# Wide attention: merged block maxima in fp32, rounded by ScalarE and turned one unit later

## The reference, cut to what matters

```python
B, S, D_MODEL = (4, 1024, 128)
NUM_HEADS, HEAD_DIM = (16, 64)
q, k, v = split_heads(x @ w_q), split_heads(x @ w_k), split_heads(x @ w_v)
attn = jnp.einsum('bnqd,bnkd->bnqk', q, k) * HEAD_DIM ** (-0.5)
attn = jax.nn.softmax(attn, axis=-1)
o = jnp.einsum('bnqk,bnkd->bnqd', attn, v)
```

## Time and profile before

| | |
|---|---|
| median of 3 runs | 3791.35 us (3790.73 to 3795.37) |
| profiled execution | 3790.09 us, of which the span is 3788.5 us |
| busy in the span | TensorE 2937.9 us (78%), VectorE 2389.0 (63%), ScalarE 1842.5 (49%), POOL 1520.5 (40%) |
| wide attention's loop, 95 to 1330 us | TensorE 1202.13 us, POOL 1123.42, VectorE 807.68, ScalarE 659.68 |
| additions of POOL | 448, 2.35 us each |

### The profile page before, as it was taken

The page is one execution under the profiler, slowest core; times in us unless marked ns, Lnnn a source line. Parts: engine busy times, 40 slices in busy tenths (PEclk is TensorE's granted clock), DMA queues, the critical chain, the costliest instruction groups (busy, mean ns, idle before and its releaser), DMA issues. The chain is left out here.

```text
span 3788.5 us, 67132 instructions
## 1 busy us (share of the span) xinstructions
PE 2937.9 (78%) x21195; PEld 1318.0 (35%) x21196; DVE 2389.0 (63%) x3399; ACT 1842.5 (49%) x2929; POOL 1520.5 (40%) x1110
## 2 busy tenths in 40 slices
PE   3999999999999953899645999999579420839983
PEld 1333333333333353333321222222246320526661
DVE  5666666666666535888857898999433454334532
ACT  2555555555555500444633898898534430443331
POOL 0899898989989910100000000101046307520000
PEclk9999999999999976999856999999789755969955
DMA  2011111111111151100023222222111212130012
GB/s 79 29 44 51 44 51 44 50 39 44 51 44 51 37 177 56 48 1 0 2 81 95 47 56 55 48 56 53 50 50 45 63 59 93 50 94 14 8 41 64
DMA packets 269545, 195.38 MB, mean 52 GB/s; under 512 B 150485, under 2 KB 212942, under 8 KB 268488
## 3 DMA queue, kind: packets, MB, share of 16 engines
q1 hardware_dynamic: 260936, 178.09, 16.5%
q0 software_dynamic: 8512, 16.11, 1.3%
HBM read 105.02 MB, written 69.19 MB: 46 GB/s over the span
## 5 line engine op out<-in xcount | busy, mean ns | idle before, releaser
L329 POOL TENSOR_TENSOR attn_esum<-attn_esum,attn_prob 128x1024 f32<-128x1024 f32 x384 | 903.8, 2354 | 41.4 <-ACT attn_prob L480 17.9
L540 DVE TENSOR_REDUCE attn_half_max<-attn_peek 128x2 f32<-128x1024 f32 x512 | 627.5, 1226 | 398.0 <-PE attn_peek L380 394.3
L480 ACT ACTIVATE attn_prob<-attn_score 128x1024 f32<-128x1024 f32 x512 | 512.6, 1022 | 297.1 <-PE attn_score L363 297.1
L844 DVE TENSOR_REDUCE attn_half_max<-attn_peek 128x2 f32<-128x1024 f32 x512 | 588.1, 1218 | 51.2 <-PE attn_peek L763 51.2
L827 ACT ACTIVATE attn_prob<-attn_score 128x512 f32<-128x512 f32 x1024 | 556.0, 596 | 111.3 <-PE attn_score L777 98.6
L410 PE MATMUL attn_acc<-attn_prob,attn_v 128*64 128x512 f32 x2048 | 487.9, 597 | 0.1
L793 PE MATMUL attn_acc<-attn_prob,attn_v 128*32 128x256 f32 x4096 | 339.1, 404 | 8.9 <-ACT attn_out L819 7.4
L1685 POOL DMA_INDIRECT sorted_x<-attn_sent_rows,attn_send x64 | 62.7, 979 | 599.8 <-PE attn_score L777 564.5
L763 PE MATMUL attn_peek<-attn_ke,attn_qe 48*128 48x512 bf16 x1024 | 208.7, 404 | 44.2 <-DMA attn_ke<-k 32.0
L777 PE MATMUL attn_score<-attn_qe,attn_ke 49*128 49x512 bf16 x1024 | 206.7, 400 | 36.9 <-DMA attn_qe<-max 29.7
L380 PE MATMUL attn_peek<-attn_hi 64*128 64x512 f16 x1024 | 200.2, 388 | 44.2 <-DVE attn_half_max L540 44.2
(11 more groups left out here) (452 smaller groups left out, 4661.4 us busy)
## 6 DMA issues: line engine op xcount, KB each, us to landing
attn_xb<-attn_x_all SPq DMA_DIRECT2D x66, 256.0 KB, 2.5
attn_invB<-inv SPq DMA_DIRECT2D x64, 256.0 KB, 4.0
o<-attn_out SPq DMA_DIRECT2D x32, 512.0 KB, 2.7
out_o<-o SPq DMA_DIRECT2D x8, 2048.0 KB
mix_f<-picked SPq DMA_DIRECT2D x16, 512.0 KB, 7.2
experts_x<-sorted_x SPq DMA_DIRECT2D x112, 65.0 KB
attn_qe<-q SPq DMA_DIRECT2D x192, 32.0 KB
attn_ke<-k SPq DMA_DIRECT2D x192, 32.0 KB
```

The source lines that it names most:

```text
L329: nc.gpsimd.tensor_tensor(own, before, prob[:, u % NPROB, :, :], ALU.add).then_inc(added, 1)
L480: nc.scalar.activation(prob[:, u % NPROB, :, :], score[:, u % 2, :, :], ACT.Exp).then_inc(exped, 1)
L540: V.tensor_reduce(half_max[:, half, :, t], peek[:], AX.X, ALU.max, negate=True).then_inc(maxed, 1)
L844: V.tensor_reduce(half_max[:, half, PAIR * pair:PAIR * (pair + 1), t], peek[:, m % NPEEK, :, :], AX.X, ALU.max, negate=True).then_inc(maxe ...
```

## The change

`merge` writes its result as fp32 to a new buffer `both`. ScalarE copies it, rounded to bf16, into `nmax` (`round_maxima`). A new function `turn` holds the transpose; it waits for the copy, and `TURN_AT` puts it one unit behind the merge, behind the maximum of that unit. ScalarE's copy stands in front of the odd unit's exponential of the step that begins there. The merge now also waits for the copy of the item before. The stage's first merge and turn stand in the prologue, one maximum apart.

```diff
+    TURN_AT = {u + 1: c for u, c in MAX_AT.items()}
...
+        both = st.sb("both", [P, NC, heads, TPC])
...
+            def round_maxima(i, c):
+                act.wait_ge(merged, NC * i + c + 1)
+                nc.scalar.activation(nmax[:, c, 0:heads * TPC].rearrange("p (h t) -> p h t", h=heads), both[:, c, :, :], ACT.Copy
+                                     ).then_inc(rounded, 1)
...
+                    if TURN_AT.get(u) == 1:
+                        round_maxima(i, 1)
+                    elif TURN_AT.get(u) == 0 and not final:
+                        round_maxima(i + 1, 0)
                     exp(i, u + 1, first)
...
             def merge(i, c, any_before):
                 dve.wait_ge(maxed, U * i + (c + 1) * PER_HALF)
                 tiles = slice(c * TPC, (c + 1) * TPC)
-                V.tensor_tensor(nmax[:, c, 0:heads * TPC].rearrange("p (h t) -> p h t", h=heads), half_max[:, 0, :, tiles],
-                                half_max[:, 1, :, tiles], ALU.min).then_inc(merged, 1)
-                dve.wait_ge(merged, NC * i + c + 1)
+                if any_before:
+                    dve.wait_ge(rounded, NC * (i - 1) + c + 1)
+                V.tensor_tensor(both[:, c, :, :], half_max[:, 0, :, tiles], half_max[:, 1, :, tiles], ALU.min).then_inc(merged, 1)
+
+            def turn(i, c, any_before):
+                dve.wait_ge(rounded, NC * i + c + 1)
                 if any_before:
                     dve.wait_ge(shift_out, DMA * BLOCKS * (NC * (i - 1) + c + 1))
                 V.transpose(nmaxT[:, c, :], nmax[:, c, :]).then_inc(max_ready, 1)
...
+                    if TURN_AT.get(u) == 1:
+                        turn(i, 1, not first)
+                    elif TURN_AT.get(u) == 0 and not final:
+                        turn(i + 1, 0, True)
```

More of the change, by code:

```diff
@@ L203, in wide_attention_stage @@
         small = st.ps("small", [P, CH])
-        names = ("w_loaded", "w_stored", "all_hi", "all_lo", "consts", "made", "hi_ready", "lo_ready", "v_ready", "peeked", "maxed", "merged",
+        names = ("w_loaded", "w_stored", "all_hi", "all_lo", "consts", "made", "hi_ready", "lo_ready", "v_ready", "peeked", "maxed", "merged", "rounded",
                  "max_ready", "scored", "exped", "added", "weighed", "read_out", "summed", "sums_read", "inverted", "normed")
-        (w_loaded, w_stored, all_hi, all_lo, consts, made, hi_ready, lo_ready, v_ready, peeked, maxed, merged,
+        (w_loaded, w_stored, all_hi, all_lo, consts, made, hi_ready, lo_ready, v_ready, peeked, maxed, merged, rounded,
          max_ready, scored, exped, added, weighed, read_out, summed, sums_read, inverted, normed) = (st.sem(n) for n in names)
@@ L527, in _ @@
             act.wait_ge(all_lo, 3 + BATCH)
+            act.wait_ge(consts, 4)
+            round_maxima(0, 0)
             exp(0, 0, True)
@@ L569, in then @@
                 def then(u):
-                    c = MAX_AT.get(u)
-                    if c == 1:
+                    if MAX_AT.get(u) == 1:
                         merge(i, 1, not first)
-                    elif c == 0 and not final:
+                    elif MAX_AT.get(u) == 0 and not final:
                         merge(i + 1, 0, True)
+                    if TURN_AT.get(u) == 1:
+                        turn(i, 1, not first)
+                    elif TURN_AT.get(u) == 0 and not final:
+                        turn(i + 1, 0, True)
                 for s in range(STEPS):
@@ L599, in _ @@
                     merge(0, 0, False)
+                elif m == PER_HALF:
+                    turn(0, 0, False)
             iterations(dve, body)
```

## The result

The changed kernel takes 3780.24 us (median of 14 runs, 3771.61 to 3789.92) against 3791.07 us before (median of 14, 3788.29 to 3798.21): 10.8 us less. The ratio is 0.997, with a 95% interval of 0.9961 to 0.9978. Forecast were 3781.5 us and 9.8 us. The profiled execution took 3775.64 us, with a span of 3774.0. One of the 21 runs of the kernel before that stand beside four of the experiments took 7794.95 us, at a granted clock of 0.511 instead of 0.88, and the ratios leave it out.

The account below looks back on a forecast made before the run. TensorE was taken to wait about 1.0 us in almost every item for a maximum delayed behind VectorE's merge, which sits out POOL's addition. 10.1 us gained less 0.3 for late shifts gave 9.8 us: 3781.5 us, range 3777 to 3789.

Parts of the forecast that it names:

- The merge: VectorE's merge, with two SBUF inputs, still waits for POOL's running addition in fp32: 2.16 us again, gain 0.
- The size: At half 1, take_low and maximum 4 come 0.34 us earlier, so look 5 does too: 10.1 us over 30 waits.
- The late shift: Half 0's shift reaches its matmul 0.1 us late; 0.8 us of lateness are absorbed at look 5, so no cost.
- The one late shift of the beginning: In the prologue and first item the shift may be late with nothing absorbing it: 0 to 1.4 us once, 0.3 taken.
- Freed by fp32: Rival: fp32 output frees the merge to 0.17 us, look 5 no longer waits: 32 us gained, 3759.5 us; chance 0.10.
- The transpose waits for POOL: Rival: the moved transpose is held by POOL's addition, shift 1.0 us late at one half: 3 us gained, 3788.5; chance 0.06.
- Nothing gained: Rival: take_low starts no earlier, held by something the trace puts down to the transpose: 3791.35 us; chance 0.04.
- slower: Rival: second half's transpose held to 725.8 us, its shift matmul waits 2.3 us an item: 3850 us; chance 0.06 with lesser mishaps.

Follow-up runs that it names:

- the fp32 merge in its old place: Changed kernel with the transpose put back directly behind the merge, fp32 output and ScalarE's rounding kept: 3794.82 us against 3790.51 before, ratio 1.0007.
- one-input merge: Kernel before with the merge as a tensor_reduce over the two key halves, bf16 output, transpose in its old place: 3755.26 us against 3790.51, ratio 0.9908.
- the run with two units: Kernel before with half 1's transpose one unit later and half 0's two units later: 3802.24 us against 3787.85, ratio 1.0042.
- bf16 merge: Kernel before with the transpose alone moved one unit later, no ScalarE rounding: 3780.88 us against 3790.51, ratio 0.9974.
- three roundings: Changed kernel with two more ScalarE copies of the same columns in front of each rounding: 3780.01 us against 3790.94 before, ratio 0.9973.

## Why the prediction was right

**The merge.** Predicted: held as before, in fp32 as in bf16. It was, 1610 ns on average against 1664 and 0.03 us behind POOL's addition. Here the rule of the Trainium skill ("SBUF — State Buffer", "Who interferes with whom") was the one that counted, for the trace of before was silent on the fp32 form; the traces of the changed kernel and of the fp32 merge in its old place now agree with it. The one-input merge took 171 ns beside the same additions; the same section of the Trainium skill says that a VectorE instruction with at most one SBUF input (outside some fast modes) does not contend, and the trace agrees. It is another instruction as well (a reduction), so by itself it doesn't isolate the input. Two readings narrow this down: take_low, with one of two inputs in PSUM, is not held either (686 ns in the changed kernel), and the narrow stage's merge, the same instruction with two inputs in SBUF, takes 176 ns where POOL adds nothing. A merge of two inputs with one of them in PSUM was not run, so that it is the second SBUF input, and not the kind of instruction, is argued and not isolated. That it is POOL's running instruction which holds the merge is shown, by the additions cut in two.

**The size.** Predicted: 0.34 us an item, from take_low starting 0.08 us before the merge's end. It started 0.08 before it, and an item became 0.346 us shorter. The remaining wait was said to be 0.65 us; it is 0.66. The count was a little high: 30 places by the list of waits, where 28 items became shorter. With the start's 0.3 us the trace shows 9.4 us for the forecast's 9.8, and the medians 10.8.

**The late shift.** Predicted: 0.1 us late at half 0 in each item, and absorbed. It came in time instead: the waits name it once in the stage. The transpose started 0.09 us before the maximum's end, not behind it (698.03, where the maximum ends at 698.12), and the second unit of delay, 1.95 us more from one maximum to the next, made TensorE late by 1.6, so the margin was 0.35 us. The step that was mis-sized is the way from the transpose's end to the shift: 4.1 us in the prediction, with 1.6 borrowed from another small load, and 3.74 us (the median of 31 places) in the run with two units, where the matmul starts as soon as the shift is there; 3.88 in the item shown there. That 0.8 us are absorbed was right, as the run with two units shows. VectorE at half 0 in the changed kernel, as the earlier trace rows:

```profile
694.06 1.23 DVE L553 TENSOR_REDUCE attn_half_max<-attn_peek 128x2 f32<-128x1024 f32 x1 [0.72 <-PE attn_peek L382]
695.41 1.21 DVE L560 TENSOR_TENSOR attn_both<-attn_half_max 128x8 f32<-128x8 f32 x1
696.89 1.23 DVE L553 TENSOR_REDUCE attn_half_max<-attn_peek 128x2 f32<-128x1024 f32 x1 [0.27 <-PE attn_peek L382]
698.03 0.20 DVE L566 STREAM_TRANSPOSE attn_nmaxT<-attn_nmax 128x32 bf16<-128x32 bf16 x1
```

The maximum behind this merge waits for its look, so nothing was to be gained here, as said.

**The one late shift of the beginning.** It was there, 1.5 us in the third item. The prediction had it in the prologue or the first item, bounded it by 1.4 us once, and took 0.3. Counted from the first merge of half 1, the changed kernel was 1.28 us behind the one before at the third item's merge and 0.29 at the fourth's. That this is the 0.3 taken is luck: it was chosen between nothing and 1.4, and in the two other kernels with both transposes one unit later and the merge still held, the same count gives 0.08 us ahead (bf16 merge) and 0.08 behind (three roundings). Timelines of TensorE and of SyncE:

```profile
160.98 0.39 PE L365 MATMUL attn_score<-attn_shift,attn_sel 64*128 64x512 bf16 x2 [1.50 <-DMA attn_shift<-max]
```

```profile
155.25 1.30 SPq L263 DMA_DIRECT2D max<-attn_nmaxT  x4
159.26 0.51 SPq L267 DMA_DIRECT2D attn_shift<-max  x2
```

From the first store to the first load 4.0 us pass, against 2.2 in the earlier trace rows. In between runs a transfer of 16 KB of the queue that the view names instruction, from 156.98 us to 157.86. From 155 to 158 us the view of the queues has:

```profile
q8 instruction: 1, 0.02, 1.8%
```

Over the eleven kernels, 23 of the 704 ways from store to load take more than 2.4 us, and in 20 of these such a transfer starts on the way; in the other 681 it does so in 3. All 23 start before 176 us, in the first three items. Whether that transfer holds up SyncE or only falls into the same time was not tested.

**The rivals.** "Freed by fp32" fell with the merges' length, but its price was right: 1.16 us an item forecast, 1.18 when the one-input merge frees it. "The transpose waits for POOL" fell: 63 of the 64 run in the middle of an addition and take 199 ns on average, at most 213. The trace of before could have told that already: 60 of its 64 lie inside an addition as well, and take 212. "Nothing gained" and "slower" fell with the time. The slower case's premise, that lateness at a shift matmul costs once it is past what is absorbed, held in the two-unit run, at half 0.

## What to carry to other kernels

Where a VectorE instruction of a few columns takes more than a microsecond, as the merge's 8 columns did here, look for a POOL instruction that ends where it ends. For this merge with two SBUF inputs another output type did not help; a form with one input did (35 us), and shorter POOL instructions helped as far as POOL had time to spare (20 us). What stands behind such an instruction in its engine's queue, and isn't needed by the next in the critical row, was worth its own length and the wait ahead of it, 0.21 and 0.13 us an item, and no more.

## What was not expected

The merges of the changed kernel last 1610 ns on average and not 1664. Most of this is a later start: 30 of the 64 start 0.12 to 0.13 us behind their maximum instead of 0.03 (as the one at 695.41 above, behind a maximum that ends at 695.29) and end with POOL's addition all the same, so that those of half 1 last 2.05 and 2.15 us by turns. The two other kernels with the fp32 merge show the same 30, those with the bf16 merge none. The fp32 merge also has one wait more ahead of it, for the rounding of the item before; which of the two delays it was not separated. Also, an independent VectorE instruction starts 0.08 us before the end of the one in front even if that one has been held by POOL for 2 us: the start is tied to the end of the held one, and a wait for its result (0.13 us) or for ScalarE's copy of it (0.37 us) puts a gap there.
